# Condition loaded first, conversions behind the functions, attention weights over two steps, and the last chunk's attention added to layer 2's gates

## The reference, cut to what matters

```python
def lstm(x, h0, Wx, Wh, b):            # c0 = 0; gates in the order i, f, o, g
    a = x_t @ Wx + b + h @ Wh          # for each time step t
    c = sigmoid(f) * c + sigmoid(i) * tanh(g)
    h = sigmoid(o) * tanh(c)
    ...
h1  = lstm(x, cond, L0_cond_Wx, L0_cond_Wh, L0_cond_b)
att = (h1 @ W_theta.T) @ (h1 @ W_phi.T).T / sqrt(128)    # in each batch, no softmax, no mask
x2  = x + att @ (h1 @ W_g.T)
h2  = lstm(x2, cond, L0_cond2_Wx, L0_cond2_Wh, L0_cond2_b)
out = x2 + relu(h2 @ W1 + b1) @ W2 + b2
```

## Time and profile before

| | |
|---|---|
| median of 3 runs | 414.52 us (414.26 to 414.95) |
| the profiled execution, its own time | 414.66 us |
| its span, first to last instruction | 412.7 us |
| PE busy | 392.8 us (95%) |
| PEld (weight loads) busy | 293.2 us (71%) |
| DVE busy | 273.1 us (66%) |
| ACT busy | 206.7 us (50%) |
| POOL busy | 8.1 us (2%) |
| HBM read, written | 2.87 MB, 1.05 MB |

### The profile page before, as it was taken

One profiled execution on the slowest core, in us unless ns is written; L12 is line 12 of the kernel. 1 busy time (PEld: TensorE's weight loads), 2 busy tenths in 40 slices (PEclk: granted clock), 3 DMA queues, 4 the chain that ended last, 5 costly groups with the idle time before them and its releaser, 6 DMA issues.

```text
span 412.7 us, 14901 instructions
## 1 busy us (share of the span) xinstructions
PE 392.8 (95%) x4979; PEld 293.2 (71%) x4979; DVE 273.1 (66%) x1697; ACT 206.7 (50%) x1451; POOL 8.1 (2%) x20
## 2 busy tenths in 40 slices
PE   8999999999999999999999999999999999999996
PEld 6777666677666677666689877777777777777775
DVE  5676666665666666666668776666677666676664
ACT  3666555555544555544556444444444444444442
POOL 7000000000000000000000000000000000000000
PEclk9999999999999999999999999999999999999999
DMA  5111011111011111010000100000000000000000
GB/s 159 39 21 21 6 17 19 19 19 19 2 17 19 19 19 18 3 17 14 15 15 2 27 20 6 20 19 19 19 6 13 19 19 19 19 9 10 19 19 13
DMA packets 11697, 8.20 MB, mean 20 GB/s; under 512 B 1098, under 2 KB 11130, under 8 KB 11675
## 3 DMA queue, kind: packets, MB, share of 16 engines
q1 hardware_dynamic: 10842, 6.17, 7.5%
q0 software_dynamic: 544, 1.23, 1.0%
q10 hardware_dynamic: 288, 0.52, 0.4%
HBM read 2.87 MB, written 1.05 MB: 9 GB/s over the span
## 4 chain that ended last, share of the span: by engine, by line
PE 68%; DVE 17%; ACT 9%; issue 4%; DVEq 0%; ACTq 0%
PE fbank L413 22%; PE fbank L386 9%; DVE cell L1006 6%; DVE ring L1016 5%; ACT fgate L818 5%; DVE scan L1003 5%; ACT cell L836 5%; PE bankU L630 4%; PE bankV L407 4%; PE ibank L407 4%; PE gbank L407 3%; PE bankV L482 3%; PE bankY L637 2%; PE bankY L477 2%; PE bankU L515 2%
## 5 line engine op out<-in xcount | busy, mean ns | idle before, releaser
L413 PEld LDWEIGHTS fbank<-ring,whf 128*128 128x128 f32 x508 | 75.5, 188 | 77.9 <-DVE ring L1016 74.1
L386 PE MATMUL fbank<-warm_w 128*128 128x384 bf16 x537 | 125.2, 325 | 0.1
L818 ACT ACTIVATE fgate<-fbank 128x16 f32<-128x16 f32 x254 | 46.8, 184 | 139.3 <-PE fbank L413 138.9
L413 PE MATMUL fbank<-ring,whf 128*128 128x16 f32 x508 | 99.8, 272 | 15.1 <-DVE ring L1016 8.8
L1003 DVE TENSOR_TENSOR scan<-fgate,cell 128x16 f32<-128x16 f32 x254 | 43.7, 172 | 70.5 <-ACT fgate L818 61.1
L1016 DVE TENSOR_TENSOR ring<-cell,ogate_h 128x16 f32<-128x16 f32 x256 | 44.5, 174 | 41.7 <-ACT cell L836 41.3
L836 ACT ACTIVATE cell<-cell 128x16 f32<-128x16 f32 x256 | 43.0, 168 | 54.1 <-DVE cell L1006 53.9
L1006 DVE TENSOR_TENSOR_SCAN cell<-scan 128x32 f32<-128x32 f32 x256 | 59.4, 232 | 10.0 <-ACT scan L828 1.3
L407 PE MATMUL ibank<-h_hi,wh_parts 128*128 128x16 f16 x508 | 62.0, 169 | 0.0
L407 PEld LDWEIGHTS gbank<-h_hi,wh_parts 128*128 128x128 f16 x508 | 52.2, 137 | 0.0
L1021 DVE TENSOR_TENSOR h_lo<-ring,h_hi 128x16 f16<-128x16 f32 x256 | 44.9, 175 | 8.7
(11 more groups left out here) (189 smaller groups left out, 603.1 us busy)
## 6 DMA issues: line engine op xcount, KB each, us to landing
rows_t<-rows SPq DMA_DIRECT2D x16, 128.0 KB
x_rows<-in_x_dram SPq DMA_DIRECT2D x17, 64.0 KB
out_dram<-y_sb SPq DMA_DIRECT2D x16, 64.0 KB
xres<-x2T SPq DMA_DIRECT2D x15, 64.0 KB, 1.9
xin<-x2T SPq DMA_DIRECT2D x14, 64.0 KB, 1.8
w<-in_L_ffn_W_dram POOLq DMA_DIRECT2D x2, 256.0 KB, 4.0
wh<-in_L_cond_Wh_dram ACTq DMA_DIRECT2D x1, 256.0 KB, 3.0
wx<-in_L_cond_Wx_dram ACTq DMA_DIRECT2D x1, 256.0 KB, 3.5
```

Of the source, the lines that this page charges most:

```text
L386: nc.tensor.matmul(fbank[1 - p][:, P:4 * P], warm_w[:], warm_three, start=False, stop=True, skip_group_check=True)
L413: nc.tensor.matmul(step_out(p, t, GF), whf[layer][:], ring[:, (s - 1) % STEPS, :], start=False, stop=True, skip_group_check=True).then_inc ...
L818: nc.scalar.activation(fgate[:], fbank[p][:, NB * t:NB * t + NB], ACT.Sigmoid, scale=1.0 / Z_UNIT).then_inc(f_done[layer], 1)
```

## The change

It has four parts.

1. Opening: cond is loaded on SP's queue ahead of x, and no longer on POOL's. TensorE transposes it after five (not six) warm matmuls, into `cell`; a fill goes. ScalarE's conversions of the second and third gate's weights move behind the functions of step 0.
2. The four attention weight products are cut: two in step 1's slot (`attention_scores`), two in step 2's (`attention_values`); the scaling copies (`keep_proj`) move by one step.
3. In the last iteration of layer 1 two products make `value_w`, W_g times layer 2's Wx. All the attention of chunk 0 but that over the last chunk is added to x early (`x2_base`) and projected into layer 2's gates f, g, i within the last step's slot, and o after the state. After the last state the last chunk's part comes as keys x `value_w` (`rows_of`), copied to `gate_rows`, times the scores, added to the gate banks (`attend_gate`).
4. The last chunk's rows are then made and copied in layer 2's step 0 (`row_products`, `keep_rows`), and with them what depends on them moves: chunk 0's x2 to step 1, the wait for the moved rows and `outer_pair` to steps 3 to 10, chunk 1's x2 to step 3, `attend_pair` and `late_x2` to steps 5 to 12, chunk 1's and 2's projections to steps 4 to 6 and 13 to 15. VectorE's loop of layer 1 is one iteration shorter, and its last iteration is written out.

```diff
         def _(sp):
+            sp.dma_start(cond_rows[:], cond).then_inc(cond_loaded, 16)
             sp.dma_start(x_rows[:, 0, :], x_ctb[0]).then_inc(rows_loaded[0], 16)
...
-                sp.wait_ge(rows_kept, c + 3 + (c == NCH - 1))
+                sp.wait_ge(rows_kept, c + 3)
...
-            keep_warm(6)
+            keep_warm(5)
+            pe.wait_ge(cond_loaded, 16)
+            pe.wait_ge(ident_ready, 2)
+            nc.tensor.transpose(cell[:, P:P + NB], cond_rows[:], ident[0:NB, 0:NB]).then_inc(cond_transposed, 1)
...
             top_product(0, fbank[1][:, 0:P])
-            fill(1, 1)
-            pe.wait_ge(cond_loaded, 16)
-            nc.tensor.transpose(bankY[:, 0:NB], cond_rows[:], ident[0:NB, 0:NB]).then_inc(cond_transposed, 1)
...
                 if first and s == 1:
-                    attention_weights()
+                    attention_scores()
                 if first and s == 2:
+                    attention_values()
...
+                if before_last and t == 1:
+                    nc.tensor.matmul(bankY[:, 2 * P:4 * P], wg_rows[:], wx[1][:, 2 * P * p:2 * P * p + 2 * P],
+                                     start=True, stop=True).then_inc(value_w_ready, 1)
+                if before_last and t == 4:
+                    pe.wait_ge(value_w_kept, p + 1)
...
-                    due = {3: (GG,), 5: (GI,), 7: (GO,)}
+                    due = {3: (GG,), 5: (GI,), 6: (GO,)}
...
+                    attended = early_attention(rows[:, p, D:2 * D], 0, 0, 2 * P)
+                    if last:
+                        attended.then_inc(base_ready, 1)
+                if last and t == 7:
+                    project_gate(1, 0, GF, x2_base[:])
+                    fill(p, 1)
+                    pe.wait_ge(o_done[0], T)
+                    project_gate(1, 0, GG, x2_base[:])
+                    project_gate(1, 0, GI, x2_base[:])
...
             score_products(0, last_keys, 0, P).then_inc(scores_ready, 1)
...
+            rows_of(GG, bankU[:, 0:P])
+            rows_of(GI, fbank[1][:, 0:P])
+            project_gate(1, 0, GO, x2_base[:])
             pe.wait_ge(scores_kept, NCH + 1)
-            early_attention(rows[:, 0, D:2 * D], 0, 0, P).then_inc(early_attn_ready, 1)
...
-            pe.wait_ge(x2_first, 1)
-            project_gate(1, 0, GG, x2T[:, 0, :]).then_inc(g_ready[1], 1)
...
+            rows_of(GO, bankY[:, 0:P])
+            pe.wait_ge(gate_rows_act, 1)
+            attend_gate(GG).then_inc(g_ready[1], 1)
+            rows_of(GF, bankU[:, 0:P])
+            pe.wait_ge(gate_rows_dve, 1)
+            attend_gate(GI).then_inc(i_ready[1], 1)
+            pe.wait_ge(gate_rows_act, 2)
+            attend_gate(GO).then_inc(o_ready[1], 1)
             bias_gate(1, 1, GF)
+            pe.wait_ge(gate_rows_dve, 2)
+            attend_gate(GF).then_inc(f_ready[1], 1)
...
                 if s == 0:
+                    row_products(1, bankY)
+                if s == 1:
                     nc.tensor.matmul(bankU[:, 0:D], hist[:, 0, :], proj[:, 1, :], start=True, stop=True
                                      ).then_inc(rows0_ready, 1)
+                    fill(0, 2)
+                    pe.wait_ge(rows_kept, NCH + 2)
+                    pe.wait_ge(o_done[1], 2)
+                    early_attention(rows[:, 0, D:2 * D], 0, 0, P).then_inc(early_attn_ready, 1)
...
+                if s == 3:
                     pe.wait_ge(rows0_kept, 1)
+                    pe.wait_ge(rows_moved[1], 16 * (ITER + 1))
+                    pe.wait_ge(rows_moved[0], 16 * (ITER + 2))
+                if 3 <= s < 3 + NB // 2:
+                    outer_pair(s - 3)
+                if s == 3:
                     pe.wait_ge(scores_kept, NCH + 2)
-                    fill(0, 2)
-                    pe.wait_ge(o_done[1], 2)
+                    pe.wait_ge(o_done[1], 4)
                     early_attention(rows[:, 0, D:2 * D], 0, P, P)
                     early_attention(rows0[:], P, P, P).then_inc(early_attn_ready, 1)
-                if s == 2:
-                    pe.wait_ge(rows_moved[1], 16 * (ITER + 1))
-                    pe.wait_ge(rows_moved[0], 16 * (ITER + 2))
...
             for s in range(STEPS):
                 step(1, s, s, opening=s == 0)
                 if s == 0:
+                    keep_rows(0, ITER, NCH)
...
+                if s == STEPS - 2:
+                    dve.wait_ge(base_ready, 1)
+                    nc.vector.scalar_tensor_tensor(out=x2_base[:], in0=xT[:, 0, :], scalar=1.0 / Z_UNIT,
+                                                   in1=bankV[:, 0:P], op0=ALU.mult, op1=ALU.add
+                                                   ).then_inc(base_kept, 1)
```

More of the change, by code:

```diff
@@ L397, in top_product, with step @@
                 nc.tensor.matmul(out, ones[:], w_diag[:], start=True, stop=True).then_inc(top_ready[layer], 1)
-            def step(layer, s, count, o_parts=None, after_seeds={}, x2_read=None):
+            def step(layer, s, count, o_parts=None, after_seeds={}, x2_read=None, base_read=False):
                 p, t = s // CH, s % CH
@@ L530, in beside1 @@
                 elif no_history:
-                    fill(0, (0, 0, 2, 2, 3, 0, 4, 3)[s])
+                    fill(0, (0, 2, 0, 2, 3, 0, 4, 3)[s])
+                elif before_last and t == 1:
+                    fill(p, 1)
+                elif last and t >= 6:
+                    fill(p, 1)
                 else:
@@ L644, in _ @@
                 if s > 0:
-                    step(1, s, s, x2_read=2 if s == 2 else None,
+                    step(1, s, s, x2_read={2: 1, 4: 2}.get(s),
                          after_seeds={2: {GG: 3 * NCH + 1, GI: 3 * NCH + 2}, 3: {GO: 3 * NCH + 3},
@@ L666, in _ @@
-                if s == 2:
-                    project_gate(1, 1, GF, x2T[:, 1, :])
[L668 to L671, removed]
+                if s == 4:
+                    pe.wait_ge(x2_first, 2)
+                    project_gate(1, 1, GF, x2T[:, 1, :])
+                if 5 <= s < 5 + NB // 2:
+                    attend_pair(s - 5)
+                if 4 <= s < 7:
+                    pe.wait_ge(seeded, 3 * NCH + 3)
+                    pe.wait_ge(o_done[1], s + 1)
+                    last = project_gate(1, 1, SEEDED[s - 4], x2T[:, 1, :])
+                    if s == 6:
+                        last.then_inc(x2_projected, 1)
@@ L672, in _ @@
+                if s in (11, 12):
+                    if s == 11:
                         pe.wait_ge(p_kept, NB // 2)
-                    for j in ((0,), (1,), (2, 3))[s - 10]:
+                    for j in ((0, 1), (2, 3))[s - 11]:
                         last = ffn_up(0, j)
@@ L677, in _ @@
                 if s == 13:
+                    pe.wait_ge(x2_done, NB // 2)
                     bias_gate(1, 0, GF)
[L679 to L691, removed]
+                    fill(1, 2)
+                    pe.wait_ge(seeded, 3 * NCH + 6)
+                    pe.wait_ge(o_done[1], 14)
                     project_gate(1, 0, GG, x2T[:, 2, :])
                     project_gate(1, 0, GI, x2T[:, 2, :])
[L694 to L697, removed]
                 if s == 14:
+                    project_gate(1, 0, GF, x2T[:, 2, :])
                     residual(x2T[:, 0, :])
@@ L706, in _ @@
                     ffn_down(3).then_inc(y_ready, 2)
+                    fill(1, 2)
+                    pe.wait_ge(o_done[1], 16)
+                    project_gate(1, 0, GO, x2T[:, 2, :]).then_inc(x2_projected, 1)
             with pe.Fori(1, ITER) as i:
@@ L836, in step @@
                 nc.scalar.activation(tanhc, c_psum, ACT.Tanh).then_inc(h_inputs[layer], 1)
+                if first:
+                    high_of_first(GO)
             def keep_rows(slot, i, c, bank=bankY):
@@ L1040, in beside1 @@
                 p, t = s // CH, s % CH
-                if t == 5 and isinstance(i, int) and p == 0:
+                if t == 5 and isinstance(i, int) and i == 0 and p == 0:
                     dve.sem_inc(scores_kept, 1)
@@ L1045, in beside1 @@
                     keep_scores(2 * P)
-                if t == CH - 1 and (p == 0 or isinstance(i, int)):
-                    if isinstance(i, int):
-                        keep_first(p)
-                    else:
-                        keep_late(0, i * STEPS - CH)
-                if s == 0 and not isinstance(i, int):
+                first = isinstance(i, int) and i == 0
+                if t == CH - 1 and first:
+                    keep_first(p)
+                if t == CH - 1 and p == 0 and not first:
+                    keep_late(0, i * STEPS - CH)
+                if s == 0 and not first:
                     keep_late(1, i * STEPS - STEPS)
@@ L1093, in _ @@
                     rest_of_second(slice(2 * H, 4 * H))
-            with dve.Fori(1, ITER) as i:
+            with dve.Fori(1, ITER - 1) as i:
                 for s in range(STEPS):
```

97 lines of the change are left out of this document (58 added, 39 removed).

## The result

The changed kernel takes 416.45 us (median of 18 runs, 414.58 to 418.93), against 414.58 for the kernel before on the same chip (18 runs, 414.05 to 415.20): a ratio of 1.0049, 95% interval 1.0035 to 1.0064. It is slower, by about 2 us. I had forecast 414.9 and no difference; the result lies outside my range. The profiled execution of after took 416.70 (span 414.7), that of before 414.66.

A forecast was written before the change was run, and what follows sets the result against it. One step's latency, 1.553 us through TensorE, VectorE and ScalarE, was taken to bound the kernel and stay untouched. Terms −0.30 − 0.26 − 0.47 + 1.30 + 0.10 = +0.37 gave 414.9 us, own range 414.2 to 415.5.

The forecast's parts named there:

- the sum: Whole kernel: all charged terms together, +0.37 us, which gave 414.9.
- rival B: Opening: TensorE idles at the new wait for cond, fast clock comes later; each us of delay costs 0.5; chance 0.12.
- the moved rows: Layer 2's start: last chunk's rows land 1.28 into the slot waiting for them; 1.30 more, between 0 and 1.4.
- Opening: Up to the first state: first gate's bias 0.43 earlier, 0.30 off the state; ends 0.65 less and 0.3 more.
- Attention weights: Layer 1's steps 1 and 2: four products spread over two slots; 0.26 less, ends 0.1 and 0.31.
- Layer change: Between layer 1's last and layer 2's first state: seven matmuls with copies hidden; 0.47 less, between 0.17 and 0.67.
- rival C: Layer change: attention path waits on each copy (0.3), extra base wait costs its worst (0.13); 415.3, chance 0.08.
- The base's wait: Last iteration of layer 1: VectorE's add must precede the next output-gate passes; 0.12 charged, 0 to 0.25.
- Rest of layer 2's first sixteen steps: Layer 2's early slots: fuller side work and a wait for late sums; 0.10 more, between −0.1 and +0.3.
- VectorE's written-out iteration: VectorE's last iteration of layer 1: writing it out leaves its instructions the same; nothing charged.
- Rival A: Layer 2's start: the rows' transfer is in time, so the 1.30 falls away; 413.6, chance 0.22.

The follow-up runs named there:

- e4: The changed kernel with part 1 taken out (old opening): 416.14 us, ratio 1.0046.
- e1: The changed kernel with seven fills put ahead of the wait for the moved rows: 415.60 us, ratio 1.0029.
- e9: The changed kernel with four fills instead of two ahead of x's transpose and seven ahead of the wait for the moved rows: 415.83 us, ratio 1.0033.
- e2: The changed kernel with the wait for the moved rows and all outer pairs one step later (steps 4 to 11): 414.27 us, ratio 1.0018.
- e3: The kernel before with the new opening (part 1) alone: 414.49 us, ratio 1.0014.
- e5: The kernel before with the new opening alone and four fills instead of two ahead of x's transpose: 414.16 us, ratio 0.9995.
- e10: The kernel before with five warm matmuls instead of six and without the fill behind the scale's product: 417.20 us, ratio 1.0039.
- e8: e7 with x loaded first and cond second on SP, cond's transpose where it was before, the fill ahead of it left out: 413.60 us, ratio 0.9978.
- e7: e6 with the third attention product in step 1, output gate's initial product one step earlier, one fill less in layer 2's step 15: 413.82 us, ratio 0.9977.
- e6: The changed kernel with the old opening and the outer pairs one step later: 414.48 us, ratio 1.0003.

## Why the prediction was wrong

**The step that failed is the price of TensorE's idle time,** in the sum and in rival B. I wrote of the moved rows that the transfer "lands at S + 5.30, 1.28 into the slot, with all of TensorE standing behind the wait", and charged 1.30, the delay alone. That delay was nearly right: e4's long step is 1.07 over normal (2.62, where I had said 2.8 to 2.95). But an idle TensorE also risks its clock, and this had no term. It fell in 5 of 18 runs of after and in 6 of 12 of e4, at some 1.5 to 1.8 us a time (medians of the two groups); with work in the hole (e1, e9) or without the wait (e2) it did in none of 29. Together with the late rises below, half of after's runs are lengthened, and that puts its median 0.97 above that of the other half.

**Rival B had the right mechanism with the wrong place and size.** I put the hole at the new wait for cond, let it decide "from about 1 us", took "the hole is at most 1 us" as evidence against it, and let each us cost 0.5. Cond was no wait at all: its load on SP took 1.9 us by the DMA rows below, and the transpose stands in after's opening chain without a gap, ahead of the first gate's bias at 5.59 (before 6.28):

```profile
cond_rows<-in_cond_dram SPq DMA_DIRECT2D x1, 8.0 KB, 1.9
```

```profile
3.39 0.21 PE cell L447
...
4.78 0.38 PE bankU L452
5.16 0.43 PE fbank L407 x2
5.59 0.28 PE gbank L377 x2
```

What waits is x, issued behind cond; I had seen that x "can take a part of this", and not that a few tenths are enough. TensorE stood 0.17 to 0.58 us before x's transpose in the profiled runs of e1, e2 and e3. These kernels and after, whose profiled run shows no such gap, share that opening and have 12 of 53 runs above 416.8 at a mean clock of 0.999 or 1.0 (a late rise doesn't show in that mean: e1's profiled run has 1.0). That these twelve all rose late is inferred from e1's. With the two fills there (e5, e9) none of 17 is. e10 shows the same without the change: 0.23 us, and seven of twelve runs some 3.3 us over before's median.

That such an opening raises the chance of a late rise is shown. What decides a single run is not: e2's profile has the longest gap of all, 0.58 us, and the fast clock is there right behind it.

```profile
5.35 0.33 PE L452 MATMUL bankU<-ident,x_rows 128*128 128x128 f32 x1 [0.58 <-DMA x_rows<-in_x_dram]
5.52 0.39 PE L407 MATMUL fbank<-w_diag,ones 128*128 128x128 f32 x2
```

Nor do the runs tell the gap from the smaller amount of work ahead of it: e5's two fills give back both, and e10 takes away both. e8 doesn't help, since the gap of 0.18 in its profile stands behind the rise: its two fills ahead of that gap took 0.49, where after's took 0.85.

The Trainium skill, "TensorE: Matmul & The Clock Gate" (section "What's actually happening"), says that the moment of the rise differs between runs of one kernel and that the ramp costs under 1% of a span. Both agree with e10, where 3.3 of 414 us is 0.8%. Where 0.2% decides, as here, that is larger than any term of the sum.

**The other terms.** The runs of after at full clock and, to judge by their times, with a timely rise have a median of 415.48, just inside the forecast's own upper end of 415.5. That is 0.90 over before, where the sum had 0.37. By steps:

- Opening, −0.30 forecast: about −0.2 where its hole is filled (e5, not told from nothing), nil on the median as it is (e3). The 0.84 in after's profile is one good run: the first state of e3, e2 and e1, with the same opening, comes at 8.78, 8.56 and 9.90, and with the old one it came at 8.40 (e7) to 9.05 (e6).
- Attention weights, −0.26: −0.10 (state 0 to state 3 takes 4.88, before 4.98). The step to state 2 did become normal, but the next one is 1.71. I had called 0.53 of products in place of two fills free there; e7, with one product back, gives 1.62.
- Layer change, −0.47: the seven products run back to back as worked out (206.01 to 207.57 is 1.56, forecast 1.58) and no copy stalls them, so rival C is out. The base's wait made state 127 late by 0.18, where I charged 0.12; the gap shrank by 0.55. Together −0.37.
- Rest of layer 2's first sixteen steps, +0.10: this term is mis-sized. States 128 to 131 cost 0.07, the two fuller slots behind the long step 0.09 to 0.10 each, as forecast, but 135 to 144 cost 0.56 (e4: 0.60, all of it in the steps to states 140, 142 and 144 of 1.72, 1.74 and 1.79). I had allowed "up to 0.1" for one slot whose side work stands behind a late sum. It is three such slots, about 0.2 each, as e4's chain shows for two of them: VectorE's add, or the next block's `relu`, comes first, then over 1.2 us of matmuls (230.25 to 231.51, 233.61 to 234.86), and only then the forget gate's product.

```profile
229.74 0.47 DVE x2T L1176
...
230.25 0.49 PE fbank L377 x2
...
231.51 0.14 PE fbank L423 x2
...
233.03 0.53 DVE relu L1190 x2
...
233.61 0.71 PE bankY L682 x4
...
234.86 0.13 PE fbank L423 x2
```

- One delay I had not looked for: the step to state 129 takes 1.68, since ScalarE's copy of the rows stands ahead of the next forget gate. ScalarE's timeline:

```profile
209.04 0.37 ACT L892 COPY rows<-bankY 128x256 f32<-128x256 f32 x1 [0.55 <-PE bankY L486]
...
209.31 0.19 ACT L867 ACTIVATE fgate<-fbank 128x16 f32<-128x16 f32 x1
```

- One gain that I had put at nothing: VectorE's written-out iteration, since it "leaves its instructions the same". Behind state 144 e4 gains 0.36, of which 0.30 is one step, to state 160. It takes 1.84 or 1.85 in before, e3, e5 and e10, and 1.55 to 1.60 in every kernel with parts 2 to 4. In before's chain VectorE stands in that step twice without a wait that the profile shows, 0.40 and 0.26 us. That the written-out iteration is what took this away is not shown.

```profile
258.31 0.40 issue
258.72 0.06 DVEq L1147
```

e4, without the opening, adds up: −0.31 at the first state of that run, +0.14 to state 127, −0.55, +0.07, +1.26, +0.60 and −0.36 behind state 144 make +0.85, and its undisturbed runs lie 0.87 above the 414.50 of before.

**Rival A is refuted.** The transfer took 4.16 us in the chain of after and 4.12 in that of e4; I had read 4.5 from two indirect rows, and came near by luck: L610 had not "waited a little". In before's timeline the last of the passes ends at 212.34 and L610 starts at 212.32, so 4.65 was only an upper bound. The estimate by the Trainium skill, "DMA: Bandwidth & Descriptors" (section "Anatomy of one DMA — SWDGE (gpsimd) path"), was 2.3 us, from a fit for DMAs on GpSimd's path, where this one is issued on SP's queue; here the measurement decides.

## What to carry to other kernels

Price a hole in TensorE's work twice: its delay, and the clock that may be lost with it. The second shows in some runs only, so one profile can look clean. When a wait moves against a transfer, look for the slot at which it is in time: one step later was worth over 2 us here. And before a load is put first in a queue, look at what then comes second: x was needed at once, cond was not.

## What the runs showed of the hardware

- A stop of 1.06 us in the middle of full work was followed by 3.4 us at 1.2 GHz in one execution, and a stop of 1.02 us at the same place in another by nothing (after and e4).
- Two matmuls fewer in the opening, with a gap of 0.23 us in the profiled run, split twelve runs into two groups 3.6 us apart (e10: medians 413.97 and 417.54). The mean clock reads 0.999 or 1.0 in both, so only the lengths of the first matmuls show it.
- A move of 128 KB inside SBUF took 4.12 to 4.16 us, where 64 KB from `x2T` take 1.9; one of the latter took 3.71 in after's profile, and the step waited for it.
